# An embedding and interaction tower on one core: first rows built by TensorE, and a new order of the first slots

## The reference

```python
e = stack([tbl_f[ids[:, f]] for f in range(32)], axis=1)          # (1024, 32, 16)
x0 = xk = e
for W in (W0, W1, W2):                                            # (32, 32, 64), (32, 64, 64) twice
    xk = relu(einsum('bmd,bhd,mhk->bkd', x0, xk, W))
    outs.append(sum(xk, axis=2))                                  # 3 x (1024, 64)
h = concatenate(outs + [dense_ctx], axis=1)                       # (1024, 208)
h = relu(h @ W_top1 + b_top1); h = relu(h @ W_top2 + b_top2); y = h @ W_top3
```

## Time and profile before

| | us |
|---|---|
| median of 3 runs | 649.59 (647.13 to 650.27) |
| the profiled execution | 648.15 |
| its span | 646.3 |
| DVE busy in it | 584.3 |
| TensorE busy | 584.9 |
| POOL busy | 469.0 |
| ACT busy | 359.5 |

### The profile page before, as it was taken

How to read it: one execution, slowest core, us unless ns; L and a number is a source line. 1 busy time by engine, 2 the same in 40 slices (tenths; PEclk the granted TensorE clock), 3 DMA queues, 4 the chain that set the end, 5 groups by cost and what they waited for, 6 DMA issues and landing times.

```text
span 646.3 us, 7777 instructions
## 1 busy us (share of the span) xinstructions
PE 584.9 (91%) x2896; PEld 209.1 (32%) x2896; DVE 584.3 (90%) x327; ACT 359.5 (56%) x595; POOL 469.0 (73%) x405
## 2 busy tenths in 40 slices
PE   0078998999898989999999999999999999999998
PEld 0023332233232323333334323333334323333455
DVE  1038898999999999999999999999999999999993
ACT  0006472756646564757666475747575565736562
POOL 6676679688888888898988888888979793803011
PEclk9999999999999999999999999999999999999999
DMA  5285585728082644637280735546380826400000
GB/s 161 47 317 135 231 278 157 286 49 298 18 251 111 207 156 94 268 64 297 39 322 7 243 119 161 202 89 274 58 303 4 281 80 187 172 5 2 1 2 1
DMA packets 27138, 96.51 MB, mean 149 GB/s; under 512 B 7414, under 2 KB 12540, under 8 KB 22876
## 3 DMA queue, kind: packets, MB, share of 16 engines
q1 hardware_dynamic: 18908, 93.90, 43.5%
q0 software_dynamic: 8192, 2.11, 2.8%
HBM read 80.25 MB, written 15.73 MB: 149 GB/s over the span
## 4 chain that ended last, share of the span: by engine, by line
DVE 42%; PE 22%; issue 17%; POOL 12%; DMA 4%; SPq 2%; ACT 1%; POOLq 0%; DVEq 0%; ACTq 0%
DVE prod L485 41%; PE acca L578 9%; POOL emb L362 7%; PE accb L578 5%; POOL prod L380 3%; DMA rows<-field_dram 3%; PE acc L548 3%; PE spread L619 2%; SPq L280 2%; DMA emb<-in_table,idx 1%; POOL zin L385 1%; DVE za L489 0%; ACT zb_field L707 0%; PE spread L542 0%; POOL zin L387 0%
## 5 line engine op out<-in xcount | busy, mean ns | idle before, releaser
L362 POOL DMA_INDIRECT emb<-in_table,idx x256 | 246.4, 962 | 83.9 <-issue 66.7
L578 PE MATMUL acca<-prod,w 128*64 128x512 f32 x1024 | 229.1, 594 | 4.6 <-DVE prod L485 2.5
L578 PE MATMUL accb<-prod,w 128*64 128x512 f32 x960 | 216.4, 596 | 13.3 <-DVE prod L485 9.5
L380 POOL TENSOR_TENSOR prod<-rows,mates 128x1024 f32<-128x1024 f32 x70 | 164.5, 2384 | 13.8 <-issue 13.4
L485 DVE TENSOR_TENSOR prod<-rows,x1a 128x2048 f32<-128x2048 f32 x64 | 146.5, 2291 | 6.7 <-ACT x1a L712 3.1
L485 DVE TENSOR_TENSOR prod<-rows,x1b 128x2048 f32<-128x2048 f32 x64 | 146.6, 2293 | 2.6 <-PE acca L578 2.0
L485 DVE TENSOR_TENSOR prod<-rows,x2a 128x2048 f32<-128x2048 f32 x64 | 146.6, 2292 | 1.1 <-PE accb L578 0.8
L485 DVE TENSOR_TENSOR prod<-rows,x2b 128x2048 f32<-128x2048 f32 x64 | 146.6, 2291 | 0.6 <-remote 0.5
L578 PEld LDWEIGHTS acca<-prod,w 128*64 128x64 f32 x1024 | 71.9, 137 | 147.0 <-issue 136.8
L578 PEld LDWEIGHTS accb<-prod,w 128*64 128x64 f32 x960 | 65.5, 137 | 155.8 <-issue 122.8
L712 ACT ACTIVATE x1a<-acc 64x512 f32<-64x512 f32 x62 | 35.4, 572 | 125.9 <-PE acc L548 118.0
(11 more groups left out here) (73 smaller groups left out, 257.3 us busy)
## 6 DMA issues: line engine op xcount, KB each, us to landing
rows<-field_dram SPq DMA_DIRECT2D x30, 2048.0 KB
field_dram<-zb_field SPq DMA_DIRECT2D x32, 256.0 KB
mates<-field_dram SPq DMA_DIRECT2D x16, 512.0 KB
emb<-in_table,idx POOLq DMA_INDIRECT x256
field_dram<-zb_field SPq DMA_DIRECT2D x32, 128.0 KB
field_dram<-zb_field SPq DMA_DIRECT2D x16, 192.0 KB
rows<-field_dram SPq DMA_DIRECT2D x2, 1024.0 KB
rows<-field_dram SPq DMA_DIRECT2D x1, 1536.0 KB
```

What stands on the lines that cost most here:

```text
L362: pool.indirect_dma_start(out=emb[q % EMBS][:, j * EMB:(j + 1) * EMB], out_offset=None, in_=table, in_offset=bass.IndirectOffsetOnAxis(ap= ...
L380: nc.gpsimd.tensor_tensor(prod0[:, (q * L0 + k) % RING0, :], rows[:, slot(q, t), :], mates[:, :], ALU.mult).then_inc(s_prod0p, 1)
L578: mm = nc.tensor.matmul(acc[j % 2][side * HID:(side + 1) * HID, :], (w1 if layer == 1 else w2)[:, step, :], prod[:, (made(layer, s, half, ...
```

## The change

`EARLY` gives slots 0 to 4 new streams: (1,0)(1,1); (2,0)(2,1); (1,2)(1,3); (2,2)(2,3); (1,4)(1,5). So a slot holds one layer of one period, for the first five. Slot 5 is (1,6)(2,4) and the rest is as before. DVE orders the units of slots 1, 3 and 5 by half, then stream, then u; of the last two units of slots 0, 2 and 4 it makes first halves of both and then second halves (`feeds`, `part`), and TensorE starts on first halves.

Period 0 isn't written to DRAM: DVE builds a 0/1 matrix `pick`, ACT and DVE copy the turned fields to `field0` (half of d in each 64 partitions), TensorE makes `mates` and the 8 tiles of `rows` with two matmuls each of 64 rows by 128 columns by 512 (`pick_tile`), and ACT copies them out (`rows_out`), one half of `mates` being DVE's. SP's first list is that of period 1. The first `keep_busy` stands ahead of the first `turn_fields`, behind ten gathers; period 1 is turned after the first pair of slot 0. The five products `product0(1, k)` of DVE move from the end of slot 0 to behind six units of slot 1; two of period 2 move from POOL to DVE, behind slot 2, and the contractions of period 2 to the end of slot 2. POOL issues early gathers in threes to fives with waits for `s_picked`, `s_l0`, `s_used` between. For period 3, SP reads `rows` ahead of `mates`. In the ACT list the inputs of two subs stand together for slots 1 to 4.

At the end, the second step of the tower of periods 12 and 13 (`tower_step(3, 1)`) moves from `last_tower` to behind the first unit of slot 31, the last unit is made and contracted in two parts, the last `z3` is shared by DVE and ACT, and the bias row matmul stands ahead of the `t1b` matmuls.

The diff, cut (indentation less by four):

```diff
...
-FIRST = [(0, 2), (2, 2), (4, 1), (5, 3)]
+PICKED = [MATES, 0, 1, 2, 3, 4, 5, 6, 7]
...
+EARLY = [[(1, 0), (1, 1)], [(2, 0), (2, 1)], [(1, 2), (1, 3)], [(2, 2), (2, 3)], [(1, 4), (1, 5)]]
 def streams(j):
-    if j == 0:
-        return [(1, 0), (1, 1)]
+    if j < len(EARLY):
+        return EARLY[j]
...
 def slot_of(layer, s):
-    return max(s - 1, 0) if layer == 1 else min(s + 1, SUBS - 1)
+    return next(j for j in range(SUBS) if (layer, s) in streams(j))
+def feeds(j):
+    return j in (0, 2, 4)
 def vector_units(j):
...
-    if 1 <= j < SUBS - 1:
+    if len(EARLY) < j < SUBS - 1:
...
-    if j == 1:
+    if j in (1, 3, 5):
...
-FIELDS_AT = {(0, 3): 2}
-SUM0 = {}
+FIELDS_AT = {(0, 0): 1, (0, 3): 2}
+SUM0 = {(1, 1): [(k, 1) for k in range(L0)], (2, 3): [(k, 2) for k in range(L0)]}
...
-for q in range(2, PERIODS):
+for q in range(3, PERIODS):
...
-def stretches(q):
-    if q < 2:
-        return [(0, GATHERS, 0)]
-    if q == 2:
-        return [(0, 9, 0), (9, 4, pairs_of(0, 0, 0)), (13, 3, pairs_of(0, 0, 1))]
-    if q == 3:
-        return [(0, 5, pairs_of(0, 1, 0)), (5, 5, pairs_of(0, 1, 1))]
-    return [(0, 5, 0), (5, 5, pairs_of(2, 1, 0)), (10, 6, pairs_of(3, 0, 0))]
+SOON = 10
...
-            (30, 1): (3, 0)}
+            (30, 1): (3, 0), (31, 0): (3, 1)}
...
-def on_vector(q):
-    return q < 2
+def on_vector(q, k):
+    return q < 2 or q == 2 and k < 2
...
+    pick = h2[:, :, :].rearrange("p m b -> p (m b)")[:, 0:LENGTH]
+    field0 = zin12[1][:, 0:HALF]
...
     def x_of(layer, s):
-        return x2 if (layer, s) == (1, 1) else x1 if layer == 1 or s == SUBS - 1 else x2
+        j = slot_of(layer, s)
+        if j < len(EARLY):
+            return x2 if s % 2 else x1
+        return x1 if layer == 1 or s == SUBS - 1 else x2
...
         def list_fields(q):
-            sp.wait_ge(s_field, q + 1)
+            sp.wait_ge(s_field, q)
...
-        list_fields(0)
-        mates_in(0)
-        for g, (t, count) in enumerate(FIRST):
-            spread_rows(0, t, count, s_first[g])
...
-            mates_in(q)
+            if q != 3:
+                mates_in(q)
...
+            if q == 3:
+                mates_in(q)
...
-                ).then_inc(s_gather[q % EMBS], 16)
-        def gather_early(q):
-            for first, count, pairs in stretches(q):
-                wait_for(pool, s_used, pairs)
-                gather(q, first, count)
+                ).then_inc(s_gather_late if q == 0 and j >= SOON else s_gather[q % EMBS], 16)
...
-        gather_early(0)
+        gather(0, 0, GATHERS)
...
-        gather_early(1)
+        gather(1, 0, 3)
+        pool.wait_ge(s_picked, 1)
+        gather(1, 3, 3)
+        pool.wait_ge(s_picked, 5)
+        gather(1, 6, 3)
+        pool.wait_ge(s_l0, 3)
+        gather(1, 9, 3)
...
-        gather_early(2)
-        gather_early(3)
+        gather(1, 12, 4)
+        pool.wait_ge(s_picked, len(PICKED))
+        gather(2, 0, 3)
+        pool.wait_ge(s_used, pairs_of(0, 0, 0))
+        gather(2, 3, 3)
+        pool.wait_ge(s_turned, 2)
+        gather(2, 6, 3)
+        pool.wait_ge(s_used, pairs_of(0, 0, 1))
+        gather(2, 9, 4)
+        pool.wait_ge(s_used, pairs_of(0, 1, 0))
+        gather(2, 13, 3)
+        pool.wait_ge(s_used, pairs_of(0, 1, 1))
+        gather(3, 0, STRETCH)
...
-        gather(3, 10, 2)
+        gather(3, STRETCH, STRETCH)
+        pool.wait_ge(s_used, pairs_of(1, 0, 0))
+        gather(3, 2 * STRETCH, STRETCH)
+        pool.wait_ge(s_used, pairs_of(1, 0, 1))
...
-        for k in range(L0):
+        gather(4, 0, STRETCH)
+        for k in range(2, L0):
...
-        gather_early(4)
+        gather(4, STRETCH, STRETCH)
+        pool.wait_ge(s_used, pairs_of(2, 0, 0))
+        gather(4, 2 * STRETCH, STRETCH)
+        pool.wait_ge(s_used, pairs_of(2, 0, 1))
+        gather(4, 3 * STRETCH, STRETCH)
...
+        dve.wait_ge(s_ident, 1)
+        for c in range(2):
+            for j, count, half, first, step, times in LIST_PARTS:
+                part = c * HID * P + c * HID + half * FIELDS + 2 * j + c
+                ones_of = bass.AP(ident[:, :].tensor, part, [[P, HID], [0, times], [2, count]])
+                to = bass.AP(h2[:, :, :].tensor, c * HID * TOP2 * 2 + 8 * first, [[TOP2 * 2, HID], [8 * step, times], [1, count]])
+                last = nc.vector.tensor_scalar_max(to, ones_of, 0.0)
+        last.then_inc(s_pick, 1)
+        dve.wait_ge(s_turned, 1)
+        for d in (2, 3):
+            for f in range(2):
+                last = nc.vector.tensor_copy(field0_at(f, d), turned_at(f, d))
+        last.then_inc(s_field0v, 1)
+        dve.wait_ge(s_field0v, 1)
+        dve.wait_ge(s_field0, 1)
+        nc.vector.tensor_copy(field0[HID:P, :], field0[0:HID, :]).then_inc(s_field0v, 1)
+        dve.wait_ge(s_picked, 1)
+        nc.vector.tensor_copy(mates[:, HALF:N], picked_at[0][1][:, :]).then_inc(s_matesv, 1)
         def rows_wait(q, t):
...
-                for g, (start, _) in enumerate(FIRST):
...
-                        dve.wait_ge(s_first[g], 16)
+                dve.wait_ge(s_copied, PICKED.index(t) + 1)
...
-        def outer(layer, s, half, u):
+        def outer(layer, s, half, u, part=None):
...
+            if part == 1:
+                outer_tiles(n, layer, s, half, u, QUADS // 2, QUADS // 2).then_inc(s_prod, 1)
+                return
...
-            at = slot(q, QUADS * u)
-            xs = x_of(layer, s)[half][:, :].rearrange("q (o n) -> q o n", o=1).to_broadcast([P, QUADS, HALF])
-            nc.vector.tensor_tensor(prod[:, n % RING, :, :], rows[:, at:at + QUADS, c * HALF:(c + 1) * HALF], xs,
-                                    ALU.mult).then_inc(s_prod, 1)
+            if part == 0:
+                outer_tiles(n, layer, s, half, u, 0, QUADS // 2).then_inc(s_part, 1)
+            elif n == len(MADE) - 1:
+                for first in range(0, QUADS, QUADS // 2):
+                    outer_tiles(n, layer, s, half, u, first, QUADS // 2).then_inc(s_prod, 1)
+            else:
+                outer_tiles(n, layer, s, half, u, 0, QUADS).then_inc(s_prod, 1)
+        def outer_tiles(n, layer, s, half, u, first, count):
+            c, at = s % 2, slot(s // 2, QUADS * u + first)
+            xs = x_of(layer, s)[half][:, :].rearrange("q (o n) -> q o n", o=1).to_broadcast([P, count, HALF])
+            return nc.vector.tensor_tensor(prod[:, n % RING, first:first + count, :],
+                                           rows[:, at:at + count, c * HALF:(c + 1) * HALF], xs, ALU.mult)
...
+                s, by_d = 2 * p + 1, zin3[third(p), :].rearrange("k (b d) -> k d b", d=EMB)
+                dve.wait_ge(s_used, taken(2, s, 1, UNITS - 1))
+                nc.vector.tensor_scalar_max(by_d[:, DH:DH + DH // 2, :],
+                                            sums_alone(s)[0:HID, 0:PART].rearrange("k (d b) -> k d b", b=BT),
+                                            0.0).then_inc(s_z3v, 1)
...
-            for i, unit in enumerate(vector_units(j)):
-                outer(*unit)
+            units = vector_units(j)
+            for i, unit in enumerate(units):
+                if feeds(j) and i == len(units) - 2:
+                    for part in range(2):
+                        for last_unit in units[-2:]:
+                            outer(*last_unit, part)
+                elif not feeds(j) or i < len(units) - 2:
+                    outer(*unit)
...
-            if j == 0:
-                for k in range(L0):
-                    product0(1, k)
+                if (j, i) == (1, 5):
+                    for k in range(L0):
+                        product0(1, k)
+            if j == 2:
+                for k in range(2):
+                    product0(2, k)
...
         def turn_fields(q, towers):
-            wait_for(pe, s_field, q)
+            if q == 1:
+                pe.wait_ge(s_field0, 1)
+            wait_for(pe, s_field, q - 1)
...
-            pe.wait_ge(s_gather[q % EMBS], (q // EMBS + 1) * GATHERS * 16)
+            if q == 0:
+                pe.wait_ge(s_gather_late, (GATHERS - SOON) * 16)
+            else:
+                pe.wait_ge(s_gather[q % EMBS], ((q // EMBS + 1) * GATHERS - (q + 1) % EMBS * (GATHERS - SOON)) * 16)
...
         def outer(j, half, u):
...
-            pe.wait_ge(s_prod, max(made(*unit) for unit in units))
-            if (half, u) == (0, 0) and j >= 2:
-                pe.wait_ge(s_x2[1], j)
+            in_parts = feeds(j) and (half, u) == (1, UNITS - 1)
+            if in_parts:
+                pe.wait_ge(s_part, j + 2)
+            else:
+                pe.wait_ge(s_prod, max(made(*unit) for unit in units))
+            if (half, u) == (0, 0):
+                if j == 0:
+                    pe.wait_ge(s_copied, len(PICKED))
+                elif j in (2, 4):
+                    pe.wait_ge(s_x2[1], j)
+                    pe.wait_ge(s_z2, j)
+                elif j in (3, 5):
+                    pe.wait_ge(s_z3, j - 1)
+                elif j > 5:
```

(100 more changed lines are left out.)

91 lines of the change are left out of this document (49 added, 42 removed).

## The result

The changed kernel takes 655.25 us (median of 7 runs, 652.72 to 656.21), the kernel before beside it 648.03 (7 runs). The ratio is 1.0099, with a 95% interval of 1.0085 to 1.0113: it is 1% slower. The forecast was 646.8 with a range of 640.0 to 653.5, so it has the wrong sign and the median lies outside the range. The profiled execution took 655.25 us, its span is 653.4 (before: 648.15 and 646.3).

A forecast was written before the change was run, and what follows sets the result against it. VectorE's 256 units (563 us) were taken as the untouched bound, POOL as hidden second. Gains of 1.1 (head after waits), 0.8 (POOL) and 0.85 (tail) summed to 2.8; on the median of 649.59 that gave 646.8, range 640 to 653.5.

The forecast's parts named there:

- The picks: Head, period 0: two half matmuls on different array rows go together, 0.9 us a tile, starting at 27.8.
- the first unit: End of the head: VectorE's first unit starts at 38.9 instead of 50.49, 11.6 us earlier.
- a wait of five or more before slot 1's sixth unit: Slot 1: the sixth unit's buffer needs the first pair, which stands behind the turn of period 2; 5.3 us lost.
- The tail: End of the kernel: tower step, halves, shared `z3` and early bias row together end 0.85 us earlier.
- Unit 58 no longer waits: Unit 58, behind POOL's last product of period 4: VectorE's loss of 0.80 us goes, nothing late in its place.
- last start 64.85: Slot 1: POOL's 16 gathers for period 2 run without a gap, 1.25 us each, the last starting at 64.85.
- Slot 3 and its end: 0.7: Slot 3 and its end: VectorE's waits there cost 0.7 us of the 14.1 summed.
- still waits 2.1: Slot 5: despite two units of another stream (4.4 us) as cover, VectorE waits 2.1 us.
- The 5.3 us in slot 1: Slot 1: turn of period 2 and first pair end at 77.2 against 71.9 wanted, 5.3 us lost.
- the first rival: Slots 1 and 2: less is given back, slot 1's 5.3 shrinks to 3.2 or 0; gain 5 to 6, 644; chance 0.25.
- The second: Head: it counts in full as waits are smaller throughout, 9 us stay, 640.5; chance 0.14.
- The third: Slots 1 and 2: gathers are held until rows have passed, period 3 lands at 101 not 93.6; 654; chance 0.17.

The follow-up runs named there:

- 13 filling matmuls: Changed kernel with 13 instead of 5 useless TensorE matmul steps behind slot 0: 653.97 us, ratio 1.0106 to the kernel before.
- turns later: Changed kernel with period 2 turned behind slot 1's first pair and period 3 behind slot 2's second: 649.46 us, ratio 1.0016 to the kernel before.
- head alone: Changed kernel's head and tail, with slots, unit order, gathers and turns as in the kernel before: 651.49 us, ratio 1.004.
- turns later, all filling matmuls, `mates` in SBUF: Changed kernel with periods 2 and 3 turned one pair later and useless matmuls behind slot 0 (9) and in slots 3 and 5: 644.21 us, ratio 0.9947.
- the version without them: Changed kernel with turns one pair later and 9 useless matmuls behind slot 0, none in slots 3 and 5: 648.93 us, ratio 1.0009.
- the best version: Changed kernel with turns one pair later, period 0's `mates` in PSUM, useless matmuls behind slot 0 and in slots 3 and 5: 643.31 us, again 644.06.
- `mates` in PSUM alone: Changed kernel with `mates` of period 0 left in PSUM, read there by VectorE's five products in halves: 654.68 us, ratio 1.0092.

## Why the prediction was wrong

**Right.** The picks: two halves of a tile run on two row ranges of the array at the same time (27.45 and 27.45, the next pair 0.5 later), and the first unit starts at 38.95 (forecast 38.9). That it fits to 0.05 is partly luck: in three profiled executions with the same head (13 filling matmuls, turns later, head alone) it starts at 40.38, 40.67 and 40.78. There the granted clock from 27 to 30 us is 0.72, 0.64 and 0.61, and picks start up to 0.86 apart instead of 0.43; in after it is 1.00. In the first two slot 1 starts at 62.41 and 62.70 all the same, so these 1.5 us are not on the path. The Trainium skill, "TensorEngine Tiling (Array Packing)", Key Properties, says that such tiles are independent (the trace agrees) and that a change of tiling mode drains the engine: the last pick starts at 32.28 and layer 0 at 32.80, 0.52 apart where two picks are 0.43 apart, so a drain costs at most 0.1 here. The kind of loss was right too: a wait of five or more before slot 1's sixth unit (6.89). The tail: 10.65 us from VectorE's last product to the end, 11.46 before, 0.8 better as forecast; that this fits is luck in part, as the place of the tower step, one of its terms, is worth nothing either way. Unit 58 no longer waits.

**Wrong, the first step: "last start 64.85".** "POOL's 16 gathers for it follow without a gap" was right; that each takes 1.25 us was not. Three lie beside VectorE's products with both operands in SBUF and take 1.78 to 1.97: 2.7 us late, last start 67.51. The kernel before had such gathers, and I read only their mean (962 ns in the earlier trace rows). The timeline of before shows them beside the products of periods 0 and 1 (not every gather there: those at 43.73 and 44.98 take 0.95 and 0.96):

```profile
41.74 1.68 POOL L362 DMA_INDIRECT emb<-in_table,idx  x1 [0.30 <-issue]
...
75.28 1.78 POOL L362 DMA_INDIRECT emb<-in_table,idx  x1 [0.30 <-issue]
```

The Trainium skill has the rule, which I didn't weigh: "GPSIMD Engine Reference", Specifications and Key points, names contention with VectorE's instructions that have two SBUF inputs. The trace agrees, with 0.94 against 1.97, and the run with one operand in PSUM shows it. The landing then took 6.9 us beneath the rows instead of the 6.01 of the earlier trace rows: 74.38 instead of 70.9. From there the working holds (turn and pair 6.3 forecast, 80.41 - 74.38 = 6.03 measured). It makes slot 1 start at 62.44 instead of 61 and unit 17 at 92.69 instead of 89.65: 3.0 of the 9.3 us by which unit 49 was missed. In slot 0 a second slip hides half of it: the 2.5 us to the landing count from a gather's start, and the prediction added them to 46.1, the end of the last gather of period 1, not to its start at 44.8. Measured: start 47.53, turn 50.04, 2.5 later; forecast landing 48.6.

**Wrong, the second and larger step: "Slot 3 and its end: 0.7" and "still waits 2.1" in slot 5.** Together 2.8; measured 7.75 (0.86, 1.21, 0.92, 1.14, 1.88, 0.53, 1.21). With the clock held at 1.00 (turns later, all filling matmuls, `mates` in SBUF) the same slots wait 3.8 (0.77, 0.67, 1.88, 0.44): 4.0 of the difference go with the clock, 1.0 was too little even at full speed. Unit 25, slot 3's first, is at 115.08, 3.6 late (my terms give 89.65 + 17.6 + 2.3 + 1.7 + 0.25 = 111.5); unit 49 is 9.3 late, so 5.7 arise in slots 3 to 5. I walked through VectorE's waits there and took TensorE at full speed. In before its pairs came one at a time in these slots, with 0.21 to 0.93 of waiting. In the changed order TensorE waits 3.68, 2.46 and 3.57 us until both streams of a quarter are made, and its clock falls: three groups of 32 take 25.83 instead of 21.27, 4.6 us more. The filling matmuls take this away and give 3.0 at unit 49 in the traces, where the version without them had two slow groups, and 4.7 by the medians (4.0 by the ratios). I had charged the clock in slot 1 alone, 2.2. The one row I had for it is a wait of 8.48 ahead of 6.73 instead of 4.56; before has no fall behind its shorter waits, so no row gave the price of one of 2.5 to 3.7 us. The question was not asked for each slot of the new order.

**What the forecast didn't consider.** The 5.3 us in slot 1 were forecast as a loss and were no necessity. They hang on one table, `FIELDS_AT`. What stays in the best version are the gaps at the starts of slots: 4.02 ahead of slot 1, 1.57 ahead of slot 3 and 1.88 in slot 5. Its first unit is 10.6 earlier than before (39.91), its unit 49 only 3.9 (165.12).

**The rivals.** None came true for this kernel. Once the order and the clock are mended, 643.3 to 644.2 is reached, the first rival's number (644), but not on its terms: the gathers of period 2 still land 6.6 us after their start (67.56, turn at 74.18), and the clock stays up only with the waits filled. The second (the head counts in full, 640.5) was not reached. The third named 98 as the landing of period 3 from which the turn of it holds TensorE. It landed at 98.46 in after and cost 0.75 there, since slot 1 was late already; with slot 1 mended it cost 2.04 and 3.48, and VectorE 4.02. Its price, 654, is near the 655.25, for another reason than the one that came true; that is luck. Its rule, that gathers are held until the rows have passed, does not hold as such: rows still moved at 392 GB/s from 98 to 100 us when period 3 was turned. Where a turn waited for them, the last gathers issued beneath rows were there 5.4 to 7.4 us after their start, most of them 6.5 to 7.0, against 2.3 to 2.6 on idle queues. Period 2's landing in after (74.38) does lie behind the end of the rows (135 GB/s from 72 to 74 us), so that one fits the rule. Two landings per run can't tell what sets this.

**Open.** `mates` in PSUM alone turns period 2 2.3 us earlier and keeps 1.1 of it at unit 49. In its trace the two pairs behind that turn take 9.13 instead of 8.39, and those behind the first wait of 2.46 8.78 instead of 8.57, so the clock takes a part; in period 1 the earlier gathers find TensorE busy (turn at 49.72 against 50.04). The later first unit (40.09) is not the reason, as runs with `mates` in SBUF and a first unit at 40.38 and 40.67 start slot 1 at 62.41 and 62.70. What makes the clock fall at the picks, or behind a wait of 2.46, in one execution and not in another stays open.

## What to carry to other kernels

When an order of work is made finer, ask for every new wait of TensorE how long it stands idle and at which clock the next group then runs, in each stage and not only in the one with the largest wait: here three of four idle stretches of 2.5 to 3.7 us cost 1.4 to 1.7 us each on top of the wait, and useless matmuls in them gave 4.0 to 4.7 us back. Put a step that waits for a DMA behind the work that is already there, not ahead of it: moving it by one pair was worth 5.8 us. A mean duration in a group (962 ns) can hide two populations (0.94 and 1.97 us), and a moved operation may land in the other one. Where the executions of one kernel run at different mean clocks, compare those at the same clock too: a part worth 1.0 us showed as 0.1 in the medians.

## What the runs showed of the hardware

- A gather's issue on POOL takes 0.94 us, and up to 1.97 beside VectorE's 128x1024 products that read both operands from SBUF (1.78, 1.97 and 1.97 beside those of period 0 in after; two such gathers in before stay at 0.95 and 0.96). Beside products and units that read one operand from PSUM it stays at 0.94 or 0.95.
- Two matmul instructions of 64 rows and 512 columns on different halves of the array start together, and the next two start 0.43 us later in a stream.
- TensorE's granted clock fell to the lower level behind idle stretches of 2.46, 3.57 and 3.68 us in slots 3 and 5 of after (0.57 from 122 to 126 us). It did not behind another of 2.46 (1.00 from 174 to 180), and stayed at 1.00 where 4 and 2 steps of `keep_busy` stood in them.
- The last gather beneath a 4 MB rows transfer is there 5.4 to 7.4 us after its start, mostly 6.5 to 7.0; on idle queues it is 2.3 to 2.6.
